# A macaron block on one core: attention matmul inside layer 4, spread of the states behind the gate

## The reference

```python
def ffn(x):      # W: ternary weights, s: one scale per output
    h = silu(lin(x, w1)) * lin(x, w2)      # 128 -> 512   ("layer 1")
    h = gelu(lin(h, h1))                    # 512 -> 512   ("layer 2")
    h = gelu(lin(h, h2))                    # 512 -> 512   ("layer 3")
    return lin(h, w3)                       # 512 -> 128   ("layer 4")

def attn(x):     # a recurrence over the 512 tokens, 16 states
    xB = x @ B
    h_t = tanh(xB_t + h_{t-1} @ A.T)
    return (hs @ C) @ W_out.T + b_out

x = x + 0.5 * ffn(layernorm(x))
x = x + attn(layernorm(x))
x = x + 0.5 * ffn(layernorm(x))
```

## Time and profile before

| | |
|---|---|
| median of 3 runs | 440.8 us |
| profiled execution | 441.55 us |
| its span in the profile | 439.7 us |
| TensorE matmul busy | 398.6 us, 91% |
| VectorE busy | 325.2 us, 74% |
| ScalarE busy | 234.4 us, 53% |
| GpSimd busy | 163.0 us, 37% |
| mean granted TensorE clock | 0.99 of full speed |

### The profile page before, as it was taken

One profiled execution on the slowest core, in us unless ns is written; L12 is line 12 of the kernel. 1 busy time (PEld: TensorE's weight loads), 2 busy tenths in 40 slices (PEclk: granted clock), 3 DMA queues, 4 the chain that ended last, 5 costly groups with the idle time before them and its releaser, 6 DMA issues.

```text
span 439.7 us, 6738 instructions
## 1 busy us (share of the span) xinstructions
PE 398.6 (91%) x1896; PEld 313.0 (71%) x1896; DVE 325.2 (74%) x688; ACT 234.4 (53%) x462; POOL 163.0 (37%) x152
## 2 busy tenths in 40 slices
PE   0448999999999999999999999999999999999981
PEld 0235777787878878787787878778787878777760
DVE  2467889899898989856869775968869595978511
ACT  2417646465664646456554556546464555646450
POOL 3105525244454524244433333534323343524220
PEclk9999999999999999999999999999999999999996
DMA  7900000000000000000101000010100001010001
GB/s 223 430 12 0 1 25 0 26 1 5 20 2 25 0 24 0 24 1 0 49 0 50 1 24 25 0 50 0 48 0 32 16 0 48 0 50 0 26 1 33
DMA packets 6048, 13.98 MB, mean 32 GB/s; under 512 B 1280, under 2 KB 1664, under 8 KB 5760
## 3 DMA queue, kind: packets, MB, share of 16 engines
q1 hardware_dynamic: 6016, 13.60, 8.3%
HBM read 7.31 MB, written 2.10 MB: 21 GB/s over the span
## 4 chain that ended last, share of the span: by engine, by line
PE 59%; DVE 16%; issue 14%; ACT 4%; POOL 3%; DMA 1%; SPq 0%; DVEq 0%; ACTq 0%; POOLq 0%
PE F L228 47%; PE FR L228 5%; DVE y L601 3%; DVE u L591 3%; DVE h_wide L645 2%; DVE y_lo L618 2%; PE SC L347 2%; DVE y_hi L608 2%; ACT y_hi L869 2%; PE MI L353 2%; POOL y_lo L1042 1%; DVE xnt_f L580 1%; DMA w_raw<-in_w2T 1%; PE MI L237 1%; PE FR L257 1%
## 5 line engine op out<-in xcount | busy, mean ns | idle before, releaser
L228 PE MATMUL F<-y_hi,w_hi 128*128 128x512 f32 x512 | 214.9, 420 | 7.4 <-DVE y_lo L618 4.0
L228 PE MATMUL F<-y_lo,w_hi 128*128 128x512 f32 x512 | 202.6, 396 | 0.0
L1042 POOL TENSOR_TENSOR y_lo<-y,y_hi 128x512 fp32r<-128x512 f32 x96 | 131.7, 1385 | 135.4 <-ACT y_hi L869 64.4
L866 ACT ACTIVATE y<-F,sc 128x512 f32<-128x512 f32 x112 | 77.1, 688 | 120.3 <-PE F L228 120.2
L228 PEld LDWEIGHTS F<-y_hi,w_hi 128*128 128x128 f32 x512 | 96.6, 189 | 34.7 <-issue 9.0
L228 PEld LDWEIGHTS F<-y_lo,w_hi 128*128 128x128 f32 x512 | 96.6, 189 | 19.8 <-issue 1.9
L618 DVE TENSOR_TENSOR y_lo<-y,y_hi 128x512 fp32r<-128x512 f32 x96 | 85.0, 896 | 34.3 <-ACT y_hi L869 32.1
L869 ACT ACTIVATE y_hi<-F,sc 128x512 fp32r<-128x512 f32 x112 | 76.7, 685 | 0.0
L848 ACT ACTIVATE th<-F,s1h 128x512 f32<-128x512 f32 x64 | 44.3, 692 | 33.0 <-PE F L228 20.1
L228 PE MATMUL F<-xn_hi,w_hi 128*128 128x512 f32 x127 | 54.3, 428 | 3.0 <-DVE xn_lo L586 2.9
L228 PE MATMUL F<-xn_lo,w_hi 128*128 128x512 f32 x127 | 51.2, 403 | 0.0
(11 more groups left out here) (86 smaller groups left out, 312.2 us busy)
## 6 DMA issues: line engine op xcount, KB each, us to landing
x_all<-in_xT SPq DMA_DIRECT2D x1, 2048.0 KB, 15.7
x_all<-x1c SPq DMA_DIRECT2D x8, 256.0 KB, 2.3
x_all<-lnin SPq DMA_DIRECT2D x8, 256.0 KB, 2.3
out<-outb SPq DMA_DIRECT2D x8, 256.0 KB, 2.1
x_all<-in_xtok SPq DMA_DIRECT2D x1, 1792.0 KB, 11.5
w_raw<-in_h1T SPq DMA_DIRECT2D x2, 512.0 KB, 6.0
w_raw<-in_h2T SPq DMA_DIRECT2D x2, 512.0 KB, 7.6
x_all<-in_xtok SPq DMA_DIRECT2D x1, 256.0 KB, 2.8
```

What stands on the lines that cost most here:

```text
L228: mm = nc.tensor.matmul(out, wtile(w, layer, k, m), y, start=first and i == 0, stop=last and i == len(pairs) - 1)
L866: nc.scalar.activation(y23[:, m, :], bankt[:, :], ACT.Gelu, scale=s)
L1042: pool.tensor_tensor(y_lo[:, k, :], y[:, k, :], y_hi[:, k, :].bitcast(F32), ALU.subtract).then_inc(out_sem, 1)
```

## The change

On TensorE the attention matmul moves from in front of layer 4 into it, behind input tile 2 and in front of tile 3, in all eight turns that have one. On VectorE `spread_states` moves from behind low 1 to behind low 2 and the gate of layer 1's last tile, in the same eight turns. The increment of l4_mm stays at layer 4's last matmul.

```diff
-            def layer4(g, gen):
+            def layer4(g, gen, beside=lambda k: None):
                 for k in range(KT):
                     ...
                     mm = split_mm(B4[:, :], 4, k, 0, y3_hi[:, k, :], y3_lo[:, k, :], k == 0, k == KT - 1, gen)
-                mm.then_inc(l4_mm, 1)
+                    if k == KT - 1:
+                        mm.then_inc(l4_mm, 1)
+                    beside(k)
...
                 layer3(g, 3, gen, True)
-                attention(c, c)
-                layer4(g, gen)
+                layer4(g, gen, lambda k: attention(c, c) if k == KT - 2 else None)
...
                 layer3(g, 3, gen, not last)
-                if scan is not None:
-                    attention(scan[0] - FIRST_PASS, scan[1])
-                layer4(g, gen)
+                layer4(g, gen, lambda k: attention(scan[0] - FIRST_PASS, scan[1])
+                       if scan is not None and k == KT - 2 else None)
...
                 low(g, 1, y3_hi_r, y23, y3_hi, y3_lo, y3_lo_dve)
-                spread_states(c, c)
                 low(g, 2, y3_hi_r, y23, y3_hi, y3_lo, y3_lo_dve)
                 gate(g + 1, KT - 1)
+                spread_states(c, c)
                 low(g, 3, y3_hi_r, y23, y3_hi, y3_lo, y3_lo_dve)
...
                 low(g, 1, y3_hi_r, y23, y3_hi, y3_lo, y3_lo_dve)
-                if att is not None:
-                    spread_states(att[0], att[1])
                 low(g, 2, y3_hi_r, y23, y3_hi, y3_lo, y3_lo_dve)
                 if not last:
                     gate(g + 1, KT - 1)
+                if att is not None:
+                    spread_states(att[0], att[1])
                 low(g, 3, y3_hi_r, y23, y3_hi, y3_lo, y3_lo_dve)
```

## The result

| | runs | median us | range |
|---|---|---|---|
| before | 4 | 440.62 | 440.07 to 441.01 |
| changed | 4 | 446.87 | 446.21 to 447.14 |

Ratio 1.0141, 95% interval 1.0123 to 1.0158: the change makes the kernel 5.4 to 7.0 us slower. I had forecast 3.4 us slower, 444.2, with a range up to 446.0: the direction was right, the size too small. All medians and intervals leave out two slow executions, 647.9 us of e_before_unroll and 562.9 us of e_att_k0_unroll, whose mean granted clock was 0.58 and 0.67 of full speed against 0.978 to 0.995 in the others.

A forecast was written before the change was run, and what follows sets the result against it. TensorE, busy 91% of the span, was taken to bound the kernel. Delays of 1.56 (turns 2 to 5), 0.50 (behind turn 5) and 1.36 (middle turns) sum to 3.4 us: 444.2, own range 442.5 to 445.3, 8 in 10 441.6 to 446.0.

The forecast's parts named there:

- The spread is 0.68 us of work and 1.10 of waiting for GpSimd: VectorE's spread of the states: its 1.78 us is 0.68 work, the rest a wait that low 2 would inherit.
- The third rival: VectorE's spread takes 1.78 us by itself, making the kernel 6.9 us slower, median 447.7; chance 0.08.
- Attention starts 0.06 behind the spread's end, the stall in front of it shrinks: TensorE inside layer 4, turn 2: attention at 310.43, its stall falling from 0.25 to 0.06 us.
- The middle turns cost 0.52, 0.52 and 0.32: Middle turns c = 0, 1, 2: TensorE delayed through x1c in the first two, through the transposes in the last; 1.36 us.
- From a matmul's end to a reader of its bank 0.03, so lnin starts 1.15 behind attention: Attention to VectorE's lnin: two attention records of 1.12 us plus 0.03, lnin starting at 311.58 instead of 311.08.
- From lnin's end to the transposes 0.22 in loop turns: TensorE's wait at the start of turns 2 to 5: 0.22 us, with 0.04 as the other end.
- What else hangs on VectorE is covered: Other VectorE work, 0.50 us late, priced at nothing because six layer-2 matmuls (1.4 us) and the transposes cover it.
- Behind turn 5 the whole delay of lnin counts, 0.50: Start of turn 6: TensorE already waits for xnt_f, whose VectorE chain goes back to turn 5's lnin; 0.50 us.
- 0.39 us a turn: Start of turns 2 to 5: transposes at 312.54 instead of 312.15, four times, 1.56 us in all.
- The first rival: Stall before attention goes and nothing replaces it: 2.5 to 2.9 us faster, median 438.1; chance 0.08.
- The second: Rival: late transposes offset by a shrinking later wait, layer 1's for xn_lo; no visible change, 441.4; chance 0.12.

The follow-up runs named there:

- e_before_unroll: Kernel before with turns 2 to 5 written out instead of looped on TensorE and VectorE; median 0.69 us faster, ratio 0.9967 to 0.9989.
- e_att_k0_unroll: Kernel before with attention behind layer 4's first input tile and turns 2 to 5 written out on TensorE and VectorE; 439.08 us, ratio 0.9965.
- e_pe_only: Changed kernel with the spread back behind low 1, so only TensorE's order differs from before; 5.38 us above before, ratio 1.0103 to 1.0137.
- e_att_k0_pewait: Kernel before with attention behind layer 4's first input tile and TensorE's wait for lnin put last; 0.77 us faster, ratio 0.9974 to 0.9993.

## Why the prediction was wrong in size

Step by step, in the order of the prediction:

- *The spread is 0.68 us of work and 1.10 of waiting for GpSimd.* Right. It takes 0.677 to 0.680 in all eight turns, and low 2 took the wait over. The rule of the Trainium skill (SBUF — State Buffer, Who interferes with whom) that a VectorE instruction with two SBUF inputs and a GpSimd instruction that reads SBUF exclude each other is borne out by this trace: 1.78 beside GpSimd, 0.68 without. The third rival is out, though its time, 447.7, lay nearer to the measured 446.87 than my 444.2 did. By the time alone it would have won; the length of the spread decides against it.
- *Attention starts 0.06 behind the spread's end, the stall in front of it shrinks.* Right: 0.05.
- *The middle turns cost 0.52, 0.52 and 0.32.* Right in size. Delays between one pair of transposes and the next were 0.34, 0.54 and 0.60, against 0.32, 0.52 and 0.52.
- *From a matmul's end to a reader of its bank 0.03, so lnin starts 1.15 behind attention.* Right where turns are not looped (1.17), **wrong in turns 2 to 5**: 1.50. Here the prediction failed first. I took 0.03 from an activation whose wait has nothing dear behind it. Lnin has three more waits and an address behind it, hidden under low 3 before. Moving attention made that wait the last one and brought 0.33 us into the open, four times. I had asked this question for TensorE's wait and not for VectorE's.
- *From lnin's end to the transposes 0.22 in loop turns.* Too low: 0.37 to 0.38, and 0.33 behind turn 1. I took the row of another wait, which has two loop-dependent waits behind it where this one has three.
- *What else hangs on VectorE is covered.* Nearly: behind c = 2, the last step of layer 2's first tile waited for y1_lo and lost 0.12, and the transposes themselves take 0.06 more when TensorE comes to them idle.
- *Behind turn 5 the whole delay of lnin counts, 0.50.* The mechanism was right: the transpose in turn 6 waits for xnt_f as before, 4.93 us later than before on the clock of the trace. With lnin's 0.33 more it is 0.8.

Turns 2 to 4 show it all in one number. I forecast 0.39 us a turn; measured are 0.92, 0.89 and 0.88. 0.39 + 0.33 (lnin) + 0.16 (transposes) = 0.88. Put into the sum of 3.4: 0.50 three times, 0.3 each between the transposes of c = 2 and turn 1 and behind turn 5, 0.1 in the middle turns give 5.6, which is what the stretch and its tail of 0.2 have within 0.2.

The first rival (chain fits into 1.43 us) is out: with no wait at all in front of attention, in e_pe_only, the chain took 1.05 + 0.75 + 0.06 = 1.86 in c = 0. The second, a wait later in the turn giving back, did not happen: the period grew by the full delay, 0.89, and the wait of L228 for xn_lo is 2.9 us over the whole span in both kernels.

The range was too narrow at its upper end. I had bounded the wait on TensorE from two rows, 0.04 and 0.22, and the one on VectorE from none.

## What to carry to other kernels

When an instruction is moved behind others, ask of each wait that depends on it whether it becomes the last to be satisfied; all that the sequencer does between that wait and the instruction (further waits, register work for loop-dependent values, an address), and a loop's branch that it reaches late, moves onto the path, here 0.33 us a time on VectorE and 0.32 on TensorE. Filling a stall with later work is free only as long as the work left behind the moved instruction covers the chain that starts at it: compute that cover for every possible place and stop at the knee, here behind the first input tile.

## What the hardware showed that I had not expected

- Register work behind a late wait costs time: three steps of 0.04 to 0.08 us and the gaps between them made 0.36 us between attention and lnin, against 0.03 in written-out turns.
- A wait turned to the last place cost 0.09 to 0.12 us more than one in the first place in the middle turns and turn 1 on VectorE (attention to lnin 1.16 or 1.17, then 1.25 to 1.28), 0.09 on TensorE in the middle turns, and gained 0.31 on TensorE in turns with loop values. I have no explanation for the loss.
- The loop's COMPARE_BRANCH took 0.21 us on TensorE's sequencer each time the loop went on, and 0.08 when it ended (e_att_k0_pewait).
- The attention's two records take 1.12 us when TensorE waits for it and 1.02 when it comes to it without a stall.
- With the same order of instructions up to there, the start of the kernel in single profiled executions came out between 204.74 and 206.25 us (the first slot behind layer 3 in c = 0, e_pe_only and before): a difference of 1.5 us that has nothing to do with the change, and the reason to compare stretches.
